# A decoder layer on one core: v and cross attention as whole 128x128 products, TensorE without its loop, new orders of work

## What is computed

```
x = x + causal_attention(layernorm(x)) @ Wout.T      # 16 heads of 16, no mask but the causal one
h = layernorm(x)
s = h @ ctx.T / 16 ; s = where(mask, s, -1e30)        # one head, 64 context tokens per sequence
x = x + softmax(s) @ ctx                              # 0 where a sequence has no valid token
x = x + down(silu(gate) * up)                         # bit_linear: rms norm, 8-bit activations,
                                                      # ternary weights, 256 -> 2*704, 704 -> 256
```

## Time and profile before

| what | value |
|---|---|
| runs | 211.62 us median of 3 (211.55 to 212.03) |
| span of the profiled execution | 212.7 us |
| TensorE clock granted, mean | 0.992 of full |
| PE / PEld busy | 194.6 / 153.5 us |
| DVE / ACT / POOL busy | 165.7 / 150.6 / 137.1 us |
| bytes moved | 12.79 MB, nearly all in the first 25 us |

### The profile page before, as it was taken

One profiled execution on the slowest core, in us unless ns is written; L12 is line 12 of the kernel. 1 busy time (PEld: TensorE's weight loads), 2 busy tenths in 40 slices (PEclk: granted clock), 3 DMA queues, 4 the chain that ended last, 5 costly groups with the idle time before them and its releaser, 6 DMA issues.

```text
span 212.7 us, 10882 instructions
## 1 busy us (share of the span) xinstructions
PE 194.6 (91%) x4104; PEld 153.5 (72%) x4107; DVE 165.7 (78%) x523; ACT 150.6 (71%) x422; POOL 137.1 (64%) x290
## 2 busy tenths in 40 slices
PE   4997999999999989999899989998999999889874
PEld 4785987978787868887787868787887866445532
DVE  1222587999988968798788888888879799999771
ACT  3468467767788886969587959887868866775821
POOL 4600341776758773948495857685755889999990
PEclk9998799999999999999999999999999999999999
DMA  5999000101010102020202011110101012000011
GB/s 172 379 330 348 25 3 6 52 3 51 6 49 30 53 6 74 0 76 2 76 0 74 2 28 48 32 44 25 51 25 51 24 52 77 0 5 26 2 43 59
DMA packets 11474, 12.79 MB, mean 60 GB/s; under 512 B 1009, under 2 KB 10801, under 8 KB 11442
## 3 DMA queue, kind: packets, MB, share of 16 engines
q1 hardware_dynamic: 11442, 12.41, 18.2%
HBM read 10.31 MB, written 2.10 MB: 58 GB/s over the span
## 4 chain that ended last, share of the span: by engine, by line
PE 72%; issue 10%; POOL 9%; DVE 4%; ACT 3%; DMA 1%; POOLq 0%; SPq 0%; DVEq 0%; ACTq 0%
PE ps L331 14%; PE ps L309 8%; PE ps L343 7%; PE ps L315 6%; PE ps L419 6%; PE ps L434 5%; PE ps L398 5%; PE ps L367 4%; PE ps L505 3%; PE ps L463 3%; POOL zh L1994 2%; PE ps L360 2%; PE ps L452 2%; PE ps L522 2%; PE ps L458 2%
## 5 line engine op out<-in xcount | busy, mean ns | idle before, releaser
L1994 POOL TENSOR_TENSOR zh<-hh,gd 128x352 f32<-128x352 f32 x32 | 31.2, 986 | 5.1 <-DVE hh L1331 4.7
L331 PE MATMUL ps<-yaT,wqk 128*128 128x128 f32 x256 | 32.9, 284 | 0.5 <-ACT yaT L681 0.5
L331 PEld LDWEIGHTS ps<-yaT,wqk 128*128 128x128 f32 x256 | 31.2, 199 | 1.2 <-ACT yaT L681 0.7
L1203 DVE TENSOR_REDUCE mx<-ps 128x16 f32<-128x1024 f32 x16 | 19.6, 1224 | 7.8 <-PE ps L367 7.6
L315 PE MATMUL ps<-wg,zT 128*128 128x352 bf16 x128 | 22.3, 312 | 0.5 <-ACT hT L681 0.4
L2016 POOL TENSOR_SCALAR hq<-zh,qh 128x704 f32<-128x704 f32 x16 | 13.6, 851 | 13.3 <-DVE qh L1360 13.0
L1910 POOL TENSOR_TENSOR rs<-ve,neghalf 128x1 f32<-128x1 f32 x32 | 20.2, 632 | 2.7
L681 ACT ACTIVATE hT<-ps 128x256 bf16<-128x256 bf16 (+1 forms) x32 | 15.5, 495 | 6.6 <-PE ps L309 6.5
L786 ACT ACTIVATE th_sb<-ps,th 128x352 f32<-128x352 f32 x32 | 17.4, 553 | 3.5 <-PE ps L315 1.8
L1318 DVE SCALAR_TENSOR_TENSOR th_sb<-th_sb,ps 128x352 f32<-128x352 f32 x32 | 16.4, 513 | 4.1 <-ACT th_sb L786 4.1
L738 ACT ACTIVATE pT<-ps 128x512 f32<-128x512 f32 x32 | 17.8, 609 | 1.3 <-PE ps L404 0.8
(11 more groups left out here) (120 smaller groups left out, 518.5 us busy)
## 6 DMA issues: line engine op xcount, KB each, us to landing
ct_in<-ctx_t SPq DMA_DIRECT2D x16, 128.0 KB, 2.1
cn_in<-ctx_n SPq DMA_DIRECT2D x16, 128.0 KB, 2.2
out<-o_out SPq DMA_DIRECT2D x16, 128.0 KB, 1.7
wg<-gate_t SPq DMA_DIRECT2D x1, 1408.0 KB, 7.7
x_in<-x SPq DMA_DIRECT2D x1, 1024.0 KB, 10.9
wd<-down_t SPq DMA_DIRECT2D x1, 640.0 KB, 8.7
wqk<-wqkv_t SPq DMA_DIRECT2D x1, 512.0 KB, 4.0
x_in<-x SPq DMA_DIRECT2D x1, 512.0 KB, 9.5
```

Of the source, the lines that this page charges most:

```text
L331: last = pe.matmul(qk_ps[:, e * P:(e + 1) * P], wqk[:, c, e * P:(e + 1) * P], yaT[:, t % 2, c, :], start=(c == 0), stop=(c == DC - 1))
L1203: V.tensor_reduce(out=mx[:, t % 2, :, 0, :], in_=scores, op=ALU.max, axis=AX).then_inc(ev["mx_d"], 1)
L1994: G.tensor_tensor(zh[:, t % 2, part], hh[:, t % 2, part], gd[:, part], ALU.mult).then_inc(ev[f"zh_d{j}"], 1)
```

## The change

- `project_v` becomes two matmuls, 128 tokens by 256 columns, both sequences at once; `keep_v` sorts the four blocks in four copies of 64 partitions by 128 columns.
- `cross_scores` becomes two matmuls of 128x128 and behind them one mask product of 128x128, which puts the large negative number on the columns of the other sequence too. Maxima and exponentials run over 128 columns, the weights are copied with one 128x128 instruction, and the doubling goes.
- The masks of all tiles are made in two GpSimd instructions (tiles 0 to 3, and 4 to 15); `mask_bf` holds all 16 and is cleared at the start; the clearing of `pxT` goes.
- The loop of TensorE goes: every call is written out, with plain numbers in the waits, and most waits that others already imply are left out. `scores_q`, `scores_k` and `readout` have 64 and 32 columns for all tiles.
- In `scores_q` the wait for q and k stands behind the causal products, in `scores_k` the wait for the maxima stands behind all products but the last eight.
- All engines have a new order. On SyncE, x groups 3 and 4 go ahead of the first context loads, and store(1), store(5), store(6) and store(10) stand ahead of the context loads of tiles 5, 9, 10 and 14. 21 matmuls without use are left in the last tiles.

```diff
-                for b in range(2):
-                    for c in range(DC):
-                        for j in range(2):
-                            last = pe.matmul(v_ps[SEQ * j:SEQ * (j + 1), b * P:(b + 1) * P], yaT[:, t % 2, c, b * SEQ:(b + 1) * SEQ],
-                                             wv[:, c, j * P:(j + 1) * P], start=(c == 0), stop=(c == DC - 1))
+                for c in range(DC):
+                    last = pe.matmul(v_ps[:, :], yaT[:, t % 2, c, :], wv[:, c, :], start=(c == 0), stop=(c == DC - 1))
                 last.then_inc(ev["v_ps"], 1)
...
             def scores_q(t, *users):
-                pe.wait_ge(ev["q_d"], at(t + 1))
-                pe.wait_ge(ev["k0_d"], at(t + 1))
-                pe.wait_ge(ev["k1_d"], at(t + 1))
                 freed(users)
...
-                        for queries in [slice(0, P)] if isinstance(t, int) else [slice(0, SEQ), slice(SEQ, P)]:
+                        for queries in halves:
...
+                pe.wait_ge(ev["q_d"], t + 1)
+                pe.wait_ge(ev["k0_d"], t + 1)
+                pe.wait_ge(ev["k1_d"], t + 1)
                 for c in range(DC):
...
             def readout(t, *users):
-                columns = SEQ if isinstance(t, int) else 32
+                columns = 32
...
-                for rows in seqs:
-                    pe.matmul(sx_ps[rows, :], row_bf, mask_bf[:, t % 2, rows], start=True, stop=False)
                 for c in range(DC):
-                    for rows in seqs:
-                        last = pe.matmul(sx_ps[rows, :], yxT[:, t % 2, c, rows], ct_in[:, t % 2, c, rows], start=False, stop=(c == DC - 1))
-                last.then_inc(ev["sx_ps"], 1)
+                    pe.matmul(sx_ps, yxT[:, t % 2, c, :], ct_in[:, t % 2, c, :], start=(c == 0), stop=False)
+                pe.wait_ge(masks_0 if t < MASKS else masks_1, 1)
+                pe.matmul(sx_ps, row_bf, mask_bf[:, t, :], start=False, stop=True).then_inc(ev["sx_ps"], 1)
...
-            with pe.Fori(0, TURNS) as turn:
-                for base in range(0, 9):
-                    at(Tile(base, turn))
-                for k in range(2):
-                    step(Tile(5 + k, turn))
-            kept.clear()
...
-                for j in range(2):
-                    rows = slice(SEQ * j, SEQ * (j + 1))
-                    last = copy(v2[rows, t % 2, :, :, j, 0:DK], v_ps[rows, :].rearrange("p (b i d) -> p b i d", b=2, i=PAIRS))
+                for b in range(2):
+                    for j in range(2):
+                        last = copy(v2[SEQ * j:SEQ * (j + 1), t % 2, b, :, j, 0:DK],
+                                    v_ps[SEQ * b:SEQ * (b + 1), j * P:(j + 1) * P].rearrange("p (i d) -> p i d", i=PAIRS))
...
-                for b in range(2):
-                    rows = slice(SEQ * b, SEQ * (b + 1))
-                    last = nc.scalar.activation(pxT[rows, t % 2, rows], pxT_ps[rows, rows], ACT.Copy, scale=2.0)
-                last.then_inc(ev["pxT_d"], 1)
+                copy(pxT[:, t % 2, :], pxT_ps).then_inc(ev["pxT_d"], 1)
```

More of the change, by code:

```diff
@@ new lines, in _ @@
+            project_qk(7)
+            transpose_h_1(1)
+            transpose_max(6)
+            project_out(5)
+            cross_scores(4)
+            transpose_h_0(1)
+            scores_k(6, ("hT_d1", 2), ("hh_d1", 3))
+            transpose_cross_weights(4, ("x1_d", 6))
+            project_v(7)
+            down(1)
+            transpose_z(3)
+            scores_q(7, ("exp_d1", 7))
+            readout(6, ("out_d", 2))
+            cross_readout(4)
+            transpose_ya(8, ("zT_d", 4))
@@ new lines, in _ @@
+            project_qk(14)
+            cross_scores(11)
+            transpose_h_1(8)
+            transpose_max(13)
+            transpose_h_0(8)
+            project_out(12)
+            scores_k(13, ("hh_d1", 10), ("hT_d1", 9))
+            project_v(14, ("expx_d", 12))
+            transpose_cross_weights(11, ("x1_d", 13))
+            down(8)
+            transpose_z(10)
+            scores_q(14, ("exp_d0", 14))
+            readout(13, ("out_d", 9))
+            transpose_ya(15, ("zT_d", 11))
@@ L678, in _ @@
+            down(14)
+            keep_busy(1, 5, ("nmx_d", 16), ("expx_d", 16))
+            transpose_h_1(15)
+            transpose_h_0(15)
+            down(15)
         @block.scalar
@@ L2281 @@
     small[:, B_ID:B_ID + P] = np.eye(P)
-    small[0, B_ROW:B_ALL] = 1
+    for b in range(2):
+        small[b, B_ROW + SEQ * b:B_ROW + SEQ * (b + 1)] = 1
     for j in range(2):
@@ L2294 @@
     wv = wqkv[:, 2 * D:].reshape(D, PAIRS, 2, DK).transpose(0, 2, 1, 3).reshape(D, D)
+    mask = np.asarray(inputs["mask_BxS2_bk0"]).reshape(tiles, 2, SEQ)
+    own = np.zeros((2, tiles, P), mask.dtype)
+    for b in range(2):
+        own[b, :, SEQ * b:SEQ * (b + 1)] = mask[:, b]
     arrays = {
```

1539 lines of the change are left out of this document (821 added, 718 removed).

## The result

The changed kernel is **slower**: 220.23 us (219.69 to 220.68, 4 runs) against 211.59 us, ratio 1.0383, 95% interval 1.0326 to 1.0440. The forecast was 206.3 us and the range ended at 209.5.

What follows compares the result with a forecast made beforehand. PE was taken to set the pace until the last tiles' attention, then a fixed tail. Terms -4.04 + 0.5 - 1.30 - 0.6 + 0.35 = -5.1, tail -0.2, took 212.7 to 207.4; less 1.1, 206.3 us; range 202.8 to 209.5.

Steps and rivals of the forecast that it cites:

- The gaps of the loop, -4.04 + 0.5: Middle steps: writing the loop out removes four readout gaps, 4.04 us; new small waits cost 0.5, between 0 and 2.
- Narrow forms, -1.30 and -0.6: Readout and scores_k outside the loop: narrower columns save 1.30 us between 20 and 57 us, 0.6 at the tail's front.
- The front gap, +0.35 (0 to 1.41): TensorE's stop near 18 us, read as late instructions: less work done before it, costing 0.35 us, at most 1.41.
- v, 0.01 a tile: project_v as whole products: nothing saved in the product, 1.02 us becoming 1.01.
- Cross scores, +0.11: cross_scores as whole products plus mask product: 0.42 us becomes 0.53, 0.11 a tile slower.
- Shape changes, -0.15 to +0.11 a tile in all, taken as 0: Around v and cross scores: fewer tile-shape changes save 0.15 a tile, offsetting slower cross scores; -2.4 to +1.8 us for 16.
- ScalarE: Four v copies take 0.86 to 1.54 us, one weights copy 214 to 428 ns; likely +0.2 us a tile beside PE.
- The tail, -0.2: Last tiles: new order with 21 useless products instead of 43 meant to be denser, DVE's work unchanged; 0.2 us saved.
- The execution the sum was made on: Baseline profile of 212.7 us: its span taken as 1.1 us above the median of the runs.
- D: Rival, whole straight-code list: late instruction blocks stop PE repeatedly, 1.41 us each; six stops give 214.8 us; chance 0.07.
- A: Rival, middle stage: other engines, DVE at 88%, hold PE back and half the gain is lost; 209.0 us; chance 0.20.
- C: Rival, loop gaps: they are waits for v and stay, leaving only the narrow columns' 1.55 us; 210.0 us; chance 0.06.

Runs made afterwards that it cites:

- w1: Kernel before with TensorE's loop written out and wide scores for all tiles, readout wide for tiles 0 to 3 only: 210.19 us, ratio 0.9912.
- w2: w1 with v and cross attention as whole products and the masks in two instructions: 214.98 us, ratio 1.0142.
- a3: Changed kernel with wide scores for all tiles and wide readout for tiles 0 to 3: 218.37 us, ratio 1.0274.
- k1: Kernel before with only TensorE's ten loop steps written out, same order, waits and widths: 211.02 us, ratio 0.9983.
- k2: Kernel before with the loop written out and narrow scores and readout for all tiles: 218.64 us, ratio 1.0324.
- h1: a3 with the last part of all four engines' lists in the order of before: 217.38 us against 218.37.
- k3: k2 plus v and cross attention as whole products and the masks in two instructions: 220.85 us, ratio 1.0361.
- p4: Changed kernel with the bulk loads held behind the first readout: 226.64 us.
- p3: k2 with the bulk loads held behind the first readout: 221.60 us.
- p1: w2 with 96 already satisfied waits ahead of TensorE's first instructions: 217.26 us.
- p5: w2 with 19 warm-up products of 48 columns instead of 7 of 128: 218.72 us.
- p6: w2 with v of tiles 0 to 3 in quarters again: 213.86 us, ratio 1.0098.

## Why the prediction was wrong

By its own steps, with the medians as the ladder: before to w1 -1.8 us (same chip), w1 to w2 +4.8, w2 to a3 +3.4, a3 to the changed kernel +1.9; together +8.3 of the 8.6 measured. **The step that failed is the same in the three terms that follow: the sum let straight code, and more instructions for the same work, be free for TensorE everywhere but at one place in the front.** The runs show a block of 256 instructions that can come late at every boundary.

**The gaps of the loop, -4.04 + 0.5: right in themselves, and the largest failure for what replaced them.** By the starts of the groups the gaps were 4.0 us of nine steps, they went, and the small waits grew by 0.7 where I had charged 0.5. But in k1 late blocks brought 3.9 us back, and a step takes 11.30. The sum has nothing for them in the middle. w1 has no late block in its steps, but its wide forms take 2.3 us longer, so there the term is worth 0.15 us a step (11.27 to 11.12), 1.3 for nine. The loop had not paid for blocks at all: its code was fetched once. "0 to 2" for new waits bounded only the waits for other engines.

**Narrow forms, -1.30 and -0.6: wrong in sign.** The groups are shorter, as read. But narrow forms are more instructions for the same work, and each 256 of them need a block. k2 against k1 is +7.6 us, 6.3 of it before project_qk(3); in the changed kernel it is +1.9 (a3).

**The front gap, +0.35 (0 to 1.41).** The reading was right: instructions that arrive late while weights load. The size was not: 1.10 + 2.31 us of idle time and 6.8 us at half clock; project_qk(3) comes 4.3 us later than in w1. I had priced a stop at its idle time alone, without the clock that falls behind it, though the profile before had that too. And I held the stop for one place, where it may come at every 256th instruction.

**v, 0.01 a tile: right**; it went from 1.02 to 0.96 us, over nine steps 9.22 to 8.67 between starts. **Cross scores, +0.11: nearly right**, 0.41 to 0.57, +0.16. **Shape changes, -0.15 to +0.11 a tile in all, taken as 0: right**; w1 and w2 have steps of 11.12 and 11.13. The clear loss of w2 is not in the products but in where they moved a boundary.

**ScalarE:** four copies of v at 275 ns are 1.10 us, inside of 0.86 to 1.54; the copy of the weights 279 ns, inside of 214 to 428. By line and shape, the changed kernel:

```profile
L814 ACT ACTIVATE v<-ps 64x128 f32<-64x128 f32 x64 | 17.6, 275 | 2.2 <-PE ps L325 1.6
...
L814 ACT ACTIVATE pxT<-ps 128x128 f32<-128x128 f32 x16 | 4.5, 279 | 3.5 <-PE ps L434 3.4
```

**The tail, -0.2: wrong.** It is 3.5 us longer (47.6 to 51.1). Of this 1.36 are a late block at 170.4 us, in the last products of scores_k. About 1.5 are the order from scores_k(15) on, by the profiles of a3 and h1; no median shows it. That 21 products without use instead of 43 meant a denser tail was an argument from the list, not from the profile: PE idles in their place. The rest of the order's 3.4 us is some 0.23 us a step (11.13 in w2, 11.36 in a3), of which the transposes of h are a third (3.79 to 4.45 us over nine steps) and the rest is spread over several groups; none of it was tested by itself.

**The execution the sum was made on.** I said that its span was 1.1 above the median; the whole execution was about 2.9 above, with a low clock that the usual one lacks (whether it also lacks the stop, no trace shows). That error pointed the other way: with it the forecast would have been 204.5.

**The rivals.** D, with a chance of 0.07, is the one that came, and its place was named: several "issue" gaps at no fixed group. It asked for six stops of 1.41 to reach 214.8; there were five waits of 6.1 us in all, of which none is the loop's, and the clock. The argument against it, that straight code from 25 to 57 us ran at 31.50 of 32.00, was drawn from code with wide forms and idle queues, so it didn't bear on narrow forms or on full queues. In k1 late blocks took nearly the whole gain of the loop; in the front, with narrow forms, they took far more than any gain. A's picture (PE idle with others as releaser) holds in the tail alone. C's time of 210.0 is, by chance, that of w1.

**Open:** why single packets far from any bulk load are late. The one ahead of k1's stop at 84 us ran 3.25 us after TensorE had entered the block before it, the one ahead of the changed kernel's stop at 170 us 5.2 us after; loads of a context had been under way at the start of both stretches, but had ended 2 us and more before the packet, and other packets are as late with no data near (3.4 us in k3, 5.0 in p4). And where the executions of one kernel text, 3 to 11 us apart, differ.

## What to carry to other kernels

A gap that a change takes away can come back as something else: the loop's gaps came back as late blocks. So write the loop out alone and time that first. Before code is written out or split finer, count the instructions of the engine's list: each block of 256 may come late, above all where the queues are full of data or a block is used up in some 3 us, and a change that saves nothing but moves a boundary can cost 3 us. Holding transfers back to let the blocks through costs as much again if anything that stands early in another engine's list needs them.

## What the runs showed of the hardware

- An instruction block is a 16 KB packet of q8 and shares the DMA engines with data: at 15.7 us with empty queues, at 18.7 us with 1.36 MB in flight in the 4 us before, for the same program. Held loads of 1.6 MB between 24 and 29 us made one of 3.83 us (p3).
- A loop of TensorE whose turn is five blocks long fetched them once: in the kernel before, no packet of q8 ran between 79.6 and 176.0 us, over four more turns.
- A block's packet ran after TensorE had entered the block before it (0.9 us after in the median in 316 packets with no data meanwhile, 5.0 at w2's late one), and TensorE used a block 1.2 us after its packet's end at the earliest (544 blocks, all kernels but the one before and p1).
- Behind a front stop the granted clock went to 0.5 (the lower of its two levels): before, 20.1 to 23.5 us, behind 1.41 us idle; w2, 22.0 to 25.4, behind 1.99; the changed kernel, 23.6 to 30.4, behind 1.10 and 2.31. h1, with 1.44 us idle at the same place, kept 1.0; so did w1, p1, p5 and p6, whose idle stretches there were of 1.13 us at most.
- A wait that is already satisfied isn't free on TensorE: 96 of them moved its start by 5.1 us (12.48 against 7.41), 53 ns each.
- A float32 record of 48 columns took 0.22 us in the warm-up, where one of 128 columns takes 0.24; each had its own weight load of 128 columns.
- Converting a mask of 2x1536 took GpSimd 1.46 us, one of 2x512 0.61 (the two of p6, 2.15 us together), one of 1x128 0.29: it goes by the columns, though less than in proportion.
